# A 32-byte spacer tile in front of the x slots: x, activations and attention tiles begin 32 bytes later

## The reference, cut to what matters

```python
x = x + ssm(layernorm(x), W_in, W_out, dt_bias, A_log, D_skip, norm_weight)
x = x + ffn(layernorm(x), w1, w2, h1, h2, w3)      # scales left out here
x = x + delta(layernorm(x), Wq, Wk, Wv, Wb, ln_w, ln_b)
x = x + ffn(layernorm(x), w1, w2, h1, h2, w3)
# ffn: h = silu(x w1) * (x w2); h = gelu(h h1); h = gelu(h h2); return h w3
```

## The kernel before, in words

| tiles | bytes past a 64-byte line before | after the change |
|---|---|---|
| all weights, `ident`, `tri`, `ones`, `stri` | 0 | 0 |
| `d_row`, `lnw_row`, `lnb_row`, `lmask`, `umask` | 32 | 32 |
| `x_sb` | 32 | 0 |
| `xf_hi`, `xf_lo`, `hA_hi`, `hA_lo`, `hB_hi`, `hB_lo`, `hid`, `gate`, `xnf` | 0 | 32 |
| ssm: `xn`, `xT`, `sz`, `xs`, `seg`, `wx`, `xD`, `y`, `yT` | 0 | 32 |
| ssm: `phase`, `ang`, `angk`, `cosT`, `sinT`, `hat`, `bT`, `cT`, `xdt`, `hst` | 32 | 0 |
| delta: `xnd`, `uw`, `pc`, `kqT`, `kr`, `st`, `ti`, `au`, `prod`, `tbd`, `oT`, `ur` | 0 | 32 |
| delta: `ksq`, `kT`, `amv` | 32 | 0 |

## Time and profile before

### The profile page before, as it was taken

One profiled execution on the slowest core, in us unless ns is written; L12 is line 12 of the kernel. 1 busy time (PEld: TensorE's weight loads), 2 busy tenths in 40 slices (PEclk: granted clock), 3 DMA queues, 4 the chain that ended last, 5 costly groups with the idle time before them and its releaser, 6 DMA issues.

```text
span 2564.4 us, 61597 instructions
## 1 busy us (share of the span) xinstructions
PE 2281.9 (89%) x25057; PEld 2034.3 (79%) x25088; DVE 1363.8 (53%) x3348; ACT 1118.9 (44%) x2160; POOL 841.3 (33%) x1003
## 2 busy tenths in 40 slices
PE   4679998887899988998999989999889999899888
PEld 3558887776888878887888878888788887897788
DVE  4565374465636555466644657356563655445531
ACT  3346332552335733365334743357333663333323
POOL 3123333323333333332323333342333333233233
PEclk8789999988999999999999999999999999999999
DMA  7000000000000001000010000100010000000000
GB/s 251 1 1 1 1 18 19 1 1 5 27 22 1 1 19 31 6 1 3 18 32 4 1 3 18 35 2 1 9 40 7 1 1 18 24 4 18 17 11 9
DMA packets 85468, 43.84 MB, mean 17 GB/s; under 512 B 69936, under 2 KB 80048, under 8 KB 85168
## 3 DMA queue, kind: packets, MB, share of 16 engines
q1 hardware_dynamic: 81504, 28.11, 4.4%
q0 software_dynamic: 3664, 11.53, 1.4%
HBM read 27.05 MB, written 12.58 MB: 15 GB/s over the span
## 4 chain that ended last, share of the span: by engine, by line
PE 61%; DVE 22%; issue 7%; POOL 5%; ACT 2%; DMA 2%; DVEq 0%; SPq 0%; POOLq 0%; ACTq 0%
PE F L1277 29%; PE Q L1336 5%; DVE ti L1127 4%; PE F L1257 4%; DVE prod L1125 3%; PE Q L1407 3%; PE F L1299 2%; PE Q L1393 2%; POOL hA_lo L586 2%; DVE hid L937 2%; PE Q L1370 2%; PE Q L1434 2%; POOL rn L638 2%; PE Q L1502 2%; PE Q L1348 1%
## 5 line engine op out<-in xcount | busy, mean ns | idle before, releaser
L586 POOL TENSOR_TENSOR hA_lo<-hid,hA_hi 128x256 fp32r<-128x256 f32 (+1 forms) x384 | 357.9, 934 | 723.8 <-ACT hA_hi L715 414.7
L1277 PE MATMUL F<-hA_hi,h_sb 128*128 128x256 f32 x2048 | 514.7, 291 | 8.6 <-DVEq L940 4.3
L1277 PE MATMUL F<-hB_hi,h_sb 128*128 128x256 f32 x2048 | 510.5, 289 | 2.1 <-POOL hB_lo L586 1.5
L1277 PE MATMUL F<-hA_lo,h_sb 128*128 128x256 f32 x2048 | 498.3, 283 | 0.0
L1277 PE MATMUL F<-hB_lo,h_sb 128*128 128x256 f32 x2048 | 496.0, 282 | 0.0
L1277 PEld LDWEIGHTS F<-hA_hi,h_sb 128*128 128x128 f32 x2048 | 392.4, 192 | 20.3 <-DVEq L940 5.7
L1277 PEld LDWEIGHTS F<-hB_hi,h_sb 128*128 128x128 f32 x2048 | 390.9, 191 | 12.8 <-POOL hB_lo L586 4.3
L1277 PEld LDWEIGHTS F<-hA_lo,h_sb 128*128 128x128 f32 x2048 | 393.3, 192 | 1.7 <-issue 1.4
L1277 PEld LDWEIGHTS F<-hB_lo,h_sb 128*128 128x128 f32 x2048 | 391.6, 191 | 0.5 <-issue 0.5
L1257 PE MATMUL F<-xf_hi,w_sb 128*128 128x256 f32 x1024 | 282.9, 310 | 81.2 <-DVEq L940 59.4
L711 ACT ACTIVATE hid<-F,sh_sb 128x256 f32<-128x256 f32 x256 | 121.3, 474 | 407.3 <-PE F L1277 405.5
(11 more groups left out here) (196 smaller groups left out, 4146.6 us busy)
## 6 DMA issues: line engine op xcount, KB each, us to landing
h_sb<-h_dram POOLq DMA_DIRECT2D x2, 4096.0 KB, 24.2
x_sb<-x_dram SPq DMA_DIRECT2D x8, 512.0 KB, 4.4
a_scr<-amv SPq DMA_DIRECT2D x32, 128.0 KB, 2.3
au<-a_scr SPq DMA_DIRECT2D x8, 512.0 KB, 3.2
t_scr<-ti SPq DMA_DIRECT2D x8, 512.0 KB, 2.6
tbd<-t_scr SPq DMA_DIRECT2D x128, 32.0 KB, 2.0
out_dram<-x_sb SPq DMA_DIRECT2D x8, 512.0 KB, 3.0
w_sb<-w_dram POOLq DMA_DIRECT2D x3, 1024.0 KB, 9.0
```

What stands on the lines that cost most here:

```text
L586: pool.tensor_tensor(lo, hid[:, n % 2, 0:w, :], hi.bitcast(F32), ALU.subtract).then_inc(f_lo.handle, 1)
L1277: last = pe.matmul(ps[:, i * TOK:(i + 1) * TOK], w[:, k, o:o + P], part[:, k, :], start=(i == 0 and k == 0 and part is src[0]), stop=(i == ...
```

## The change

One tile of 8 float32 per partition is declared between `umask` and `x_sb`. Nothing writes or reads it. No instruction is added, removed or moved; every tile that is declared behind it starts 32 bytes later.

```diff
         lmask = sb("lmask", [P, BLK])
         umask = sb("umask", [P, BLK])
 
+        line_pad = sb("line_pad", [P, 8])
         x_sb = sb("x_sb", [P, SLOTS, NT, D])
         bst = sb("bst", [P, NT, 6])
```

## The result

The change made the kernel faster: 2549.6 us (2547.0 to 2554.1, four runs) against 2566.3 us before, a ratio of 0.9935 with a 95% interval of 0.9917 to 0.9953. The forecast was 2565.4 us and no change; the lower end of the range was 2557.

What follows compares the result with a forecast made beforehand. TensorE bounds the kernel, working 89% of the span and holding 61% of the chain. Terms sum to 0 (bounds -1.7 to +36 us): 2566.2 us for the profiled execution, 0.8 us over the median, so forecast 2565.4 us, range 2557 to 2577.

Steps and rivals of the forecast that it cites:

- TensorE's moving operand: Lines 1277 and 1257: operand now starts at a half line; weight load sets the distance, so 0, bounds 0 to +26 us.
- the comparison of tiles: Same operation and shape from a line start and a half line, set side by side by single source lines, using medians.
- The term of the weight loads: 128x128 blocks of `hat` (half line) and `y` (line start) both load in 141 ns median; line 1299 therefore gets 0.
- The rival of the clock: Slow clock stretches shift in the loop's turns: 2556.4 us if faster, chance 0.08; for the worse 0.05.
- The rival of GpSimd: Line 586 reads slower from half lines, up to 9.4 us on the chain: 2575 us, chance 0.12.
- the slower moving operand: Rival on about 6900 matmuls of lines 1277 and 1257: +26 us, 2591 us, chance 0.05.
- ScalarE, VectorE, GpSimd and the DMA terms: Each taken as 0; bounds: VectorE 0.7 us either way, GpSimd up to 9.4 us, DMA -1 to +1 us.
- the upper bounds of the terms: Most each term could add, stated together as +36 us, mostly from TensorE's moving operand and GpSimd's line 586.
- the case of the clock: Four longer turns of the loop all going the short way: -9.0 us, 2556.4 us, chance 0.08.

Runs made afterwards that it cites:

- the run over columns: TensorE alone, moving operand 128 to 512 columns wide at three places, also fewer stationary columns: 111 to 112 ns up to 224 columns, 120 at 256 (same place).
- three kernels: Against the kernel before: everything by 32 bytes, weights too, 2565.6 us; ffn tiles by 96 bytes, 2565.3; other tiles by half a line with ffn tiles by 256 bytes, 2566.8.
- five: Against before: weights alone 2548.0 us; ffn tiles alone 2549.1; ffn tiles by 192 bytes 2546.4, with `w3_sb` moved 2542.3; other tiles, first try, 2546.7.
- both its measurements: The change against the kernel before, first 2549.6 us, ratio 0.9935; once more beside the other kernels 2547.0 us, ratio 0.9912.
- the map: TensorE alone, groups of 64 float32r matmuls with stationary and moving operand at varied places, rest of the kernel left out: 113.4 to 123.1 ns a matmul.

## Why the prediction was wrong

The step that failed is TensorE's moving operand. The prediction read rows 5 as 1.90/16 = 119 ns for line 1370, found the same as line 1299's 120, and concluded that the weight load sets the distance. The length of a merged row holds the last matmul's own 280 ns; from start to start it is (1.90 - 0.28) / 15 = 108 ns. The single records of the trace are clearer still: the second matmul starts 60 ns behind the first, and every further one 110 to 112 ns behind the one ahead. The difference to 120 was there and was the whole case: the distance can go down to the flat 111 to 112 ns of the run over columns, the moved columns held it at 120, and the term had 8 ns to give. The Trainium skill, TensorE: Matmul & The Clock Gate, LDWEIGHTS (loading the stationary operand), gives the columns divided by 1.2 for a load; for 128 columns that is an estimate of 107 ns, 4 to 5 ns under the flat part. The Trainium skill, TensorE: Matmul & The Clock Gate, Back-to-back issue gap, gives N/2.4 + 2.5 for the gap of an isolated matmul at full clock, an estimate of 109 ns for 256 columns; the runs show 120 at the same place and 113.4 at best, and the measurement decides.

The bounds failed with it. The lower bound of this term was put at 0 although nothing excluded a gain: the row could only say what the distance was, not that it couldn't shrink. A gain of 3 ns on the 6900 matmuls that the prediction counted on the chain would have been -20.7 us; measured are -16.7 and -20.5. Three smaller slips changed nothing: the 122 ns of line 1277 hold the last matmul's own length too (119.7 from start to start), the upper bounds of the terms add up to 37 and not 36 us, and the case of the clock counted four longer turns where the starts show three of 303.5 us and one of 301.3.

The second failure is what the comparison of tiles asked. It set tiles at half lines beside tiles at line starts, each by itself, and rows 2, 3, 4 and 7 did stay as they were: 586, 425, 140 and 1290 ns after. But a matmul has two operands in this memory, and the place of one against the other was in no comparison. The prediction noted that this operand had no row, and still gave it the value of rows that didn't resemble it.

What held: ScalarE, VectorE, GpSimd and the DMA terms at 0 (landing times are the same as in rows 8 but for `amv`, 2.2 us instead of 2.3, the 0.1 us that the prediction had reckoned). The term of the weight loads held for the rows that it named (140 ns for `hat`), but not for what it concluded from them: line 1299, which it gave 0, went from 119.5 to 118.3 ns, 1.2 us in all, and the loads in line 1277 take 188 ns in the median instead of 192. Whether a shorter load is cause or effect of the shorter distance the runs don't tell. The rival of GpSimd didn't happen (1290 against 1287 ns), nor the slower moving operand. The rival of the clock is real but is not the cause: the mean granted clock of the profiled execution is 0.961, below the 0.965 of before. The second profiled execution of the change (2547.5 us, 0.965) settles it: the clock stood at 0.50 for 178 us in it and for 180 us before, and the four turns take 300.5, 300.1, 300.2 and 300.4 us. And the medians of the kernels sort by the distance in line 1277, at 119.7 to 119.9 within 0.1% of before (three kernels), at 117 and below 0.65 to 1.0% faster (five, and the change in both its measurements).

What stays open is the cause inside TensorE. That two reads of the same memory get in each other's way, better or worse by their phase, fits the map, the period and the two states, but is only argued, and the one test of it spoke against its simple form: with a quarter of the stationary columns the matmuls still took 118 ns.

## What to carry to other kernels

Where a kernel lives on streams of float32r matmuls with 128 stationary and 256 moving columns, the distance from start to start is worth measuring against what the weight load alone needs; a spacer between weights and activations costs nothing and gave up to 1% here. The place to try is found by a small program with TensorE alone, over at least 256 bytes of distance and with each place several times in different orders, since a place that is good for one width can be bad for another and the same place can run at two distances. And in a merged row the distance of equal instructions is the next start less the first, not the length divided by the count.

## What the runs showed of the hardware that I had not expected

Float32r matmuls of 256 columns take 113.4 to 123.1 ns from start to start by the places of their two operands and by what ran ahead of them, with TensorE alone at work, in a pattern that returns after 256 bytes. Up to 224 columns they take 111 to 112 ns and none of three places made a difference. The same places can run in two states, 113.6 and 117.8 ns, that last over 64 matmuls. Matmuls in full float32 kept their median distances in every line when the change moved their operands.
